# Heads' inverse root in a decoder block: one scale-and-add and one power on GpSimd in place of eleven chained VectorE operations

## The chip, the cores and the metric

One core of one Trainium2 chip runs the whole program. The metric is the device time in microseconds of one execution. A core has five engines with a queue each: TensorE (PE; its weight loads are listed as PEld), VectorE (DVE), ScalarE (ACT), GpSimd (POOL) and SyncE (SP), which here only issues transfers. Each engine works through its own queue in order; between engines the order is set by semaphores that the kernel writes out by hand.

## What is computed

A decoder block on x of shape (4, 256, 256): a decaying linear attention with 16 heads of 16 columns, then four routed experts, then a second small attention across the batch, each with a residual and a layer norm behind it. The part that matters here is the norm of each head behind the first attention:

```python
def _gated_group_rmsnorm(o, gate, weight):
    x = o * sigmoid(gate)
    xg = x.reshape(b, n, HEADS, HEAD_DIM)            # 16 heads of 16
    ms = mean(xg * xg, axis=-1, keepdims=True)
    xg = xg * rsqrt(ms + EPS)                        # EPS = 1e-6
    return xg.reshape(b, n, d) * weight
...
x = layernorm(x + gated_group_rmsnorm(attention) @ Wo)
x = layernorm(x + experts(x))
x = layernorm(x + second_attention(x))
```

## The kernel before, in words

The 1024 tokens lie as 8 tiles of 128 tokens, a token to a partition. The program is a software pipeline in rounds: in attention round i the engines work on tile i (scores), tile i-1 (weighted values) and tile i-2 (norm and output projection). Attention rounds are 0 to 7; rounds 8 and 9 finish the tiles 6 and 7 and already run beside the experts, whose rounds begin at round 7. Every engine has its own hand-written order within a round:

- **PE**, round i: `transpose_qk(i)`; `attend(i-1)` (L1106, L1111); in even rounds `make_state` (L1120); `proj_qkv(i+1)` (L1029); four matmuls `scores(i, g)` (L1087), of which the third and fourth wait until the first and second have been masked (their PSUM banks, 3 and 4, are used in turn); `transpose_on(i-2)` (L1024, reads the tile `on`); `turn_back(i-1)` (L1132); `project_o(i-2)` (L1029, reads `onT`, which ACT copies in L512). Then round i+1 begins with `transpose_qk`.
- **DVE**, round i: `copy_kT(i)` (L711); `gate_o(i-2)` (L733, makes `og`); `norm_o(i-2)`: the squares (L738), the sum over each head (L741, 128x16 into `oms`), and `inverse_root`; in even rounds `decay_state` (L726); `ln_apply` (L755); `rope_cos(i+1)` (L695); `mask_scores(i, 0)` and `(i, 1)` (L717); `rope_add(i+1)` (L704); `mask_scores(i, 2)` and `(i, 3)`; `residual1(i-2)` with its statistics (L762, L749, L751).
- **POOL**, round i: `sine_part(i+1)` (L284, two instructions, waits for ACT's L482); in round 7 one expert mask (L336); `scale_o(i-2)` (L292, makes `on` from `og` and `ors`); `ln_rstd(0, i-2)` (L298 and L301, an add and a power on one column); in rounds 1 to 3 `turn_keys(i)` (L317 to L326). In rounds 8 and 9 there is no sine part, and the expert masks (L336) stand behind `scale_o`.

`inverse_root` is a bit trick and three Newton steps: eleven instructions on 128x16, each waiting for the one before it through the semaphore `dve_chain`. Its last one raises `o_rstd`, on which `scale_o` waits. `inverse_root` is also called later, by `head_rstd`, on the second attention; that call isn't touched.

```python
link(eng.tensor_scalar(v, src, scale, eps, ALU.mult, ALU.add))
link(eng.tensor_scalar(dst.bitcast(I32), v.bitcast(I32), -0.5, float(0x5f3759df), ALU.mult, ALU.add))
for step in range(3):
    link(eng.scalar_tensor_tensor(out=a, in0=v, scalar=-0.5, in1=dst, op0=ALU.mult, op1=ALU.mult))
    link(eng.tensor_tensor(a, a, dst, ALU.mult))
    last = eng.scalar_tensor_tensor(out=dst, in0=a, scalar=1.5, in1=dst, op0=ALU.add, op1=ALU.mult)
```

Of the kernel before, what the change touches and what calls it, by code (L numbers as in the profile page):

```python
# [15 lines left out]
ALU = mybir.AluOpType  # L16
ACT = mybir.ActivationFunctionType
AX = mybir.AxisListType
# [3 lines left out]
P = 128  # L22
# [3 lines left out]
H, HD = 16, 16  # L26
# [5 lines left out]
LN_EPS, RMS_EPS = 1e-5, 1e-6  # L32
# [55 lines left out]
def decoder_block(nc, x, tokens, ctx, wq, wk, wv, wo, wg1, wg2, norm_w, conv_w, fwq, fwk, fwv, fwg, router, fwout,  # L88
                  consts, out):
    stack = ExitStack()  # L90
    with stack:
        def sb(name, shape, dt=F32):
            return stack.enter_context(nc.sbuf_tensor(name, shape, dt))
# [5 lines left out]
        def S_(name):  # L99

            if name not in made:
                made[name] = stack.enter_context(nc.semaphore(name))
            return made[name]
# [37 lines left out]
        oT = sb("oT", [P, 2, 512])  # L141
        og = sb("og", [P, 2, D])
        osq = sb("osq", [P, 2, D])
        oms = sb("oms", [P, H])
        ors = sb("ors", [P, 2, H])
        on = sb("on", [P, 2, D])
        onT = sb("onT", [P, 2, KT, P])
# [57 lines left out]
        half_neg = con[:, C_POW:C_POW + 1]  # L205
# [4 lines left out]
        def heads(ap, e=HD):  # L210
            return ap.rearrange("p (h e) -> p h e", e=e)
# [48 lines left out]
        def _(eng):  # L260
# [25 lines left out]

            def scale_o(i):

                eng.wait_ge(S_("o_rstd"), i + 1)
                if i >= 2:  # L290
                    eng.wait_ge(S_("onT_made"), i - 1)
                eng.tensor_tensor(heads(on[:, i % 2, :]), heads(og[:, i % 2, :]),  # L292
                                  ors[:, i % 2, :].unsqueeze(2).to_broadcast([P, H, HD]), ALU.mult)\
                   .then_inc(S_("o_normed"), 1)
# [46 lines left out]
            def attention_round(i):  # L341
                if i + 1 < TILES:
                    sine_part(i + 1)
                if i == MOE_START:
                    eng.wait_ge(S_("mask"), 6)
                    mask_part("hTe_pool", hTe, hT, 0, (VECTOR_EXPERTS_H, E), "z_made", "hT_copied")
                if 0 <= i - 2 < TILES:
                    scale_o(i - 2)
                    if i < TILES:
                        ln_rstd(0, i - 2)  # L350
                if 1 <= i < L:
                    turn_keys(i)
# [279 lines left out]
        def _(eng):  # L632
# [40 lines left out]
            def link(ins):  # L673
                chain[0] += 1
                ins.then_inc(S_("dve_chain"), 1)
                eng.wait_ge(S_("dve_chain"), chain[0])

            def inverse_root(dst, src, n, scale, eps, done):

                v, a = newton[:, 0, 0:n], newton[:, 1, 0:n]  # L680
# [6 lines that stand above are left out]
                    if step < 2:  # L687
                        link(last)
                last.then_inc(S_(done), 1)
# [46 lines left out]
            def norm_o(i):  # L736
                eng.wait_ge(S_("gated"), i + 1)
                eng.tensor_tensor(osq[:, i % 2, :], og[:, i % 2, :], og[:, i % 2, :], ALU.mult)\  # L738
                   .then_inc(S_("o_squared"), 1)
                eng.wait_ge(S_("o_squared"), i + 1)  # L740
                eng.tensor_reduce(oms[:, :], heads(osq[:, i % 2, :]), AX.X, ALU.add).then_inc(S_("o_ms"), 1)  # L741
                eng.wait_ge(S_("o_ms"), i + 1)
                if i >= 2:
                    eng.wait_ge(S_("o_normed"), i - 1)
                inverse_root(ors[:, i % 2, :], oms[:, :], H, 1.0 / HD, RMS_EPS, "o_rstd")

            def ln_stats(n, i, xin):
                eng.wait_ge(S_(f"ln{n}_sum"), i + 1)
# [32 lines left out]
            def attention_round(i):  # L781
# [11 lines left out]
                if 0 <= i - 2 < TILES:  # L793
                    gate_o(i - 2)
                    norm_o(i - 2)
# [563 lines left out]
```

## Time and profile before

| what | value |
|---|---|
| time, median of 3 runs | 255.02 us |
| lowest and highest run | 254.4 and 258.87 us |
| span of the profiled execution | 256.0 us |
| busy: PE, DVE, POOL, ACT | 209.2, 176.7, 114.0, 81.7 us |
| mean granted TensorE clock | 0.925 of full speed |
| instructions | 3809 |

The span runs from the first instruction to the last of one profiled execution; it is the time that the rows below add up to, 1.0 us above the median of the runs. A busy share is a mean over stages with different limits, so the stage around the change (here from about 42 to 148 us) has to be read by itself.

### The profile page before, as it was taken

How to read it: one execution, taken by the hardware profiler on the slowest of the kernel's cores; microseconds unless marked ns; L12 is line 12 of the kernel's file. 1: busy time of each engine (PE TensorE's matmuls, PEld its weight loads, DVE VectorE, ACT ScalarE, POOL GpSimd, SP SyncE). 2: the span in 40 equal slices, each digit the busy share in tenths (PEclk: the TensorE clock that was granted, in tenths of full speed). 3: DMA queues.
4: the chain of work that ended last, by engine and by line, in shares of the span. 5: the costliest groups of instructions: out<-in, count | busy, mean ns of one | idle time of the engine just before them, and what ended most of it. 6: DMA issues, size and time to landing. Idle time of an engine off the chain costs nothing.

```text
span 256.0 us, 3809 instructions
## 1 busy us (share of the span) xinstructions
PE 209.2 (82%) x1254; PEld 146.0 (57%) x1254; DVE 176.7 (69%) x438; ACT 81.7 (32%) x219; POOL 114.0 (45%) x188
## 2 busy tenths in 40 slices
PE   3788999995987798849799989999999997842461
PEld 1367555562745364515799776686786966411340
DVE  1168848779597979793556863348769788897751
ACT  0075664452432534241100113403223234423021
POOL 9661207335161413140516352346558529656352
PEclk9999999999799999977979999999999999995555
DMA  7990000000000000000000000000000001001011
GB/s 195 339 299 5 3 0 4 0 1 0 3 1 0 3 1 0 3 0 0 3 0 3 1 0 0 3 1 0 0 3 0 0 4 40 3 0 41 0 38 45
DMA packets 7027, 6.65 MB, mean 26 GB/s; under 512 B 1232, under 2 KB 6624, under 8 KB 7008
## 3 DMA queue, kind: packets, MB, share of 16 engines
q1 hardware_dynamic: 5744, 5.33, 6.6%
q10 hardware_dynamic: 1264, 1.08, 1.4%
q8 instruction: 10, 0.16, 0.3%
q14 instruction: 9, 0.07, 0.1%
HBM read 5.36 MB, written 1.05 MB: 25 GB/s over the span
## 4 chain that ended last, share of the span: by engine, by line
PE 52%; DVE 24%; issue 9%; POOL 6%; ACT 4%; DMA 3%; ACTq 1%; DVEq 0%; POOLq 0%
PE bank L1029 19%; PE bank L1230 12%; PE bank L1087 9%; PE bank L1244 4%; PE bank L1024 3%; DMA w_qk<-in_L_attn_Wk 3%; DVE hTe L776 2%; DVE w_qk L937 2%; PE bank L1132 2%; DVE stats L749 1%; POOL rstd L301 1%; DVE newton L685 1%; DVE probs L717 1%; PE bank L1120 1%; DVE newton L684 1%
## 5 line engine op out<-in xcount | busy, mean ns | idle before, releaser
L1087 PE MATMUL bank<-qx,kT 128*128 128x512 f32 x64 | 33.7, 652 | 10.6 <-DVE probs L717 8.9
L1230 PE MATMUL bank<-hTe,ctxT 128*128 128x128 f32 x256 | 31.7, 285 | 2.6 <-issue 2.6
L1230 PEld LDWEIGHTS bank<-hTe,ctxT 128*128 128x128 f32 x256 | 31.0, 201 | 3.2 <-issue 3.1
L499 ACT ACTIVATE qx<-bank,con 32x256 f32<-32x256 f32 x64 | 26.4, 458 | 16.0 <-PE bank L1024 15.4
L1244 PE MATMUL bank<-ctxT,aTe 128*128 128x256 f32 x128 | 29.0, 379 | 0.0
L284 POOL TENSOR_TENSOR rsin<-qk,rope_tab 128x256 f32<-128x256 f32 x16 | 13.2, 845 | 34.9 <-ACT qk L482 34.9
L1029 PE MATMUL bank<-f_w,oT 128*128 128x512 f32 (+4 forms) x80 | 28.0, 496 | 0.8 <-ACT oT L552 0.7
L298 POOL TENSOR_SCALAR rstd<-agg 128x1 f32<-128x1 f32 x24 | 5.3, 222 | 49.3 <-DVE agg L751 48.5
L1087 PEld LDWEIGHTS bank<-qx,kT 128*128 128x128 f32 x64 | 11.7, 197 | 26.8 <-issue 24.5
L717 DVE TENSOR_TENSOR probs<-bank,con 128x512 f32<-128x512 f32 x32 | 21.6, 686 | 5.8 <-PE bank L1087 5.0
L1244 PEld LDWEIGHTS bank<-ctxT,aTe 128*128 128x128 f32 x128 | 23.7, 190 | 2.9
L336 POOL TENSOR_TENSOR aTe<-rcos,mask 128x256 f32<-128x256 f32 x8 | 11.9, 1493 | 25.5 <-DVE rcos L835 25.5
L1029 PEld LDWEIGHTS bank<-f_w,oT 128*128 128x128 f32 x80 | 14.4, 190 | 12.0 <-issue 5.7
L835 DVE TENSOR_TENSOR rcos<-rcos,bank 128x256 f32<-128x256 f32 x8 | 3.4, 420 | 21.7 <-ACT rcos L602 21.7
L1029 PE MATMUL bank<-w_qk,xT 128*128 128x512 f32 x32 | 17.0, 658 | 1.5 <-DMA w_qk<-in_L_attn_Wk 1.5
L301 POOL TENSOR_TENSOR rstd<-rstd,con 128x1 f32<-128x1 f32 x24 | 14.0, 582 | 2.0
L336 POOL TENSOR_TENSOR hTe<-hT,mask 128x512 f32<-128x512 f32 x8 | 13.3, 1656 | 2.6 <-ACT hT L539 2.6
L1024 PE MATMUL bank<-con,fgo 128*128 128x128 f32 x16 | 3.7, 357 | 12.8 <-POOL fgo L414 12.8
L512 ACT ACTIVATE onT<-bank 128x256 f32<-128x256 f32 x8 | 3.1, 384 | 33.8 <-PE bank L1024 33.8
L1029 PE MATMUL bank<-f_out,onT 128*128 128x256 f32 x32 | 11.7, 522 | 1.6 <-ACT onT L592 1.6
L1024 PEld LDWEIGHTS bank<-con,fgo 128*128 128x128 f32 x16 | 2.4, 179 | 15.2 <-POOL fgo L414 14.8
L1111 PE MATMUL bank<-probs,v_sb 128*32 128x128 f32 x256 | 10.8, 274 | 0.0
(128 smaller groups left out, 407.7 us busy)
## 6 DMA issues: line engine op xcount, KB each, us to landing
x_sb<-in_x SPq DMA_DIRECT2D x4, 256.0 KB, 6.8
ctx_sb<-in_ctx SPq DMA_DIRECT2D x1, 1024.0 KB, 12.3
out<-x_sb SPq DMA_DIRECT2D x8, 128.0 KB, 1.7
fgo<-in_itok_BxS ACTq DMA_DIRECT2D x1, 512.0 KB, 9.3
con<-shape_constants SPq DMA_DIRECT2D x1, 338.5 KB, 3.0
w_v<-in_L_attn_Wv SPq DMA_DIRECT2D x1, 256.0 KB, 5.5
w_qk<-in_L_attn_Wq ACTq DMA_DIRECT2D x1, 256.0 KB, 5.7
w_qk<-in_L_attn_Wk ACTq DMA_DIRECT2D x1, 256.0 KB, 7.3
```

What stands on the lines that cost most here:

```text
L284: eng.tensor_tensor(dst[:, :, s, :], src[:, :, 1 - s, :], tab[:, :, s, :], ALU.mult)\
L298: eng.tensor_scalar(rstd[:, n, i:i + 1], agg[:, n, i, 1:2], LN_EPS, None, ALU.add)\
L301: eng.tensor_tensor(rstd[:, n, i:i + 1], rstd[:, n, i:i + 1], half_neg, ALU.pow)\
L336: eng.tensor_tensor(dst[:, j % 2, experts[0]:experts[1], :, :], two(src[:, j % 2, :]).unsqueeze(1).to_broadcast([P, n, KT, P]), mask[:, ex ...
L499: eng.activation(qx[rr, i % 2, :, 2 * r + par, :], two(bank[2][rr, 0:2 * P]), ACT.Copy, scale=con[rr, C_PARITY + par:C_PARITY + par + 1]). ...
L717: eng.tensor_tensor(probs[:, i % 2, 4 * g:4 * g + 4, :], bank[3 + g % 2][:, :].rearrange("p (h n) -> p h n", h=4), causal.unsqueeze(1).to_ ...
L1024: last = eng.transpose(dst[:, k * P:(k + 1) * P], src[:, k * P:(k + 1) * P], ident)
L1029: last = eng.matmul(dst, lhsT[:, k, :], w[:, k, :], start=(k == 0), stop=(k == KT - 1))
L1087: eng.matmul(bank[3 + g % 2][:, :], kT[:, i % 2, g // 2, :], qx[:, i % 2, g // 2, 4 * (g % 2):4 * (g % 2) + 4, :].rearrange("p h n -> p (h ...
L1111: last = eng.matmul(bank[5][32 * n:32 * n + 32, g * P:(g + 1) * P], v_sb[:, i % 3, h, :], probs[:, i % 2, h, :], start=(i % 2 == 0), stop= ...
L1230: last = eng.matmul(bank[0][:, f * P:(f + 1) * P], ctxT[:, k, e, f * P:(f + 1) * P], hTe[:, j % 2, e, k, :], start=(e == 0 and k == 0), st ...
L1244: last = eng.matmul(bank[3][:, 0:D], aTe[:, j % 2, e, k, :], ctxT[:, k, e, :], start=(e == 0 and k == 0), stop=(e == E - 1 and k == KT - 1))
```

## The change

The eleven operations leave VectorE. The sums of the squares, `oms`, get a second buffer, and VectorE's part ends with the sum, which raises `o_ms`. GpSimd's `scale_o` now waits for `o_ms` instead of `o_rstd`, scales and adds (`1/16` and the epsilon) into `ors`, waits for that, raises it to the power -0.5 with a column of constants spread over the 16 columns, waits for that, and then scales `og` as before. VectorE's sum waits, from the third tile on, for the power of the tile two before it.

```diff
-        oms = sb("oms", [P, H])
+        oms = sb("oms", [P, 2, H])
@@ def scale_o(i):   (GpSimd)
-                eng.wait_ge(S_("o_rstd"), i + 1)
+                eng.wait_ge(S_("o_ms"), i + 1)
+                eng.tensor_scalar(ors[:, i % 2, :], oms[:, i % 2, :], 1.0 / HD, RMS_EPS, ALU.mult, ALU.add)\
+                   .then_inc(S_("o_meansq"), 1)
+                eng.wait_ge(S_("o_meansq"), i + 1)
+                eng.tensor_tensor(ors[:, i % 2, :], ors[:, i % 2, :], half_neg.to_broadcast([P, H]), ALU.pow)\
+                   .then_inc(S_("o_rooted"), 1)
+                eng.wait_ge(S_("o_rooted"), i + 1)
                 if i >= 2:
                     eng.wait_ge(S_("onT_made"), i - 1)
                 eng.tensor_tensor(heads(on[:, i % 2, :]), heads(og[:, i % 2, :]),
@@ def norm_o(i):   (VectorE)
                 eng.wait_ge(S_("o_squared"), i + 1)
-                eng.tensor_reduce(oms[:, :], heads(osq[:, i % 2, :]), AX.X, ALU.add).then_inc(S_("o_ms"), 1)
-                eng.wait_ge(S_("o_ms"), i + 1)
                 if i >= 2:
-                    eng.wait_ge(S_("o_normed"), i - 1)
-                inverse_root(ors[:, i % 2, :], oms[:, :], H, 1.0 / HD, RMS_EPS, "o_rstd")
+                    eng.wait_ge(S_("o_rooted"), i - 1)
+                eng.tensor_reduce(oms[:, i % 2, :], heads(osq[:, i % 2, :]), AX.X, ALU.add).then_inc(S_("o_ms"), 1)
```

## Rows read from the trace of the kernel before

**Rows 1.** The page: busy time of each engine.

```profile
PE 209.2 (82%) x1254; PEld 146.0 (57%) x1254; DVE 176.7 (69%) x438; ACT 81.7 (32%) x219; POOL 114.0 (45%) x188
```

**Rows 2.** Stretches, rounds 2, 3, 5, 7, 8: length; PE, PEld, DVE, ACT, POOL busy; clock.

```profile
42.19:53.73 11.54, 11.39 (x101) 7.14 (x100) 8.73 (x24) 5.15 (x12) 3.79 (x8) 1.00 0.01 3
53.73:67.65 13.92, 11.09 (x63) 6.66 (x62) 10.65 (x25) 5.15 (x12) 5.68 (x13) 0.88 0.00 1
...
81.79:93.55 11.76, 9.68 (x63) 5.58 (x62) 9.86 (x25) 5.15 (x12) 2.94 (x5) 1.00 0.01 2
...
106.87:120.42 13.55, 10.14 (x57) 4.93 (x56) 9.22 (x24) 4.55 (x11) 3.05 (x4) 0.75 0.00 1
120.42:134.31 13.89, 11.92 (x137) 11.38 (x136) 7.92 (x21) 1.87 (x5) 4.57 (x5) 0.88 0.00 1
```

**Rows 3.** Waits of PE from 42 to 121: us in total, times, longest.

```profile
PE bank L1087 <- DVE probs L717: 8.9, 5, 2.8
```

**Rows 4.** Timeline of round 5: start, length, engine, line, tiles, [idle before].

```profile
83.19 0.22 POOL L298 TENSOR_SCALAR rstd<-agg 128x1 f32<-128x1 f32 x1 [5.28 <-DVE agg L751]
...
83.48 0.57 POOL L301 TENSOR_TENSOR rstd<-rstd,con 128x1 f32<-128x1 f32 x1
83.78 0.42 DVE L738 TENSOR_TENSOR osq<-og 128x256 f32<-128x256 f32 x1
...
84.69 0.17 DVE L681 TENSOR_SCALAR newton<-oms 128x16 f32<-128x16 f32 x1
...
87.20 0.65 DVE L686 SCALAR_TENSOR_TENSOR ors<-newton,ors 128x16 f32<-128x16 f32 x1
...
88.09 1.10 DVE L695 TENSOR_TENSOR rcos<-qk,rope_tab 128x512 f32<-128x512 f32 x1
...
89.94 1.96 PE L1087 MATMUL bank<-qx,kT 128*128 128x512 f32 x4 [2.04 <-DVE probs L717]
```

**Rows 5.** Timeline of round 2, where PE never waits.

```profile
48.15 3.85 PE L1087 MATMUL bank<-qx,kT 128*128 128x512 f32 x8
48.26 1.81 POOL L284 TENSOR_TENSOR rsin<-qk,rope_tab 128x256 f32<-128x256 f32 x2 [4.59 <-ACT qk L482]
...
50.03 0.61 POOL L292 TENSOR_TENSOR on<-og,ors 128x256 f32<-128x256 f32 x1
...
51.84 0.38 PE L1024 MATMUL bank<-con,on 128*128 128x128 f32 x2
```

**Rows 6.** GpSimd's groups by form: busy us, mean ns of one | idle before.

```profile
L301 POOL TENSOR_TENSOR rstd<-rstd,con 128x1 f32<-128x1 f32 x24 | 14.0, 582 | 2.0
...
L361 POOL TENSOR_SCALAR side<-fd 128x32 f32<-128x32 f32 x3 | 1.7, 555 | 0.2
...
L361 POOL TENSOR_SCALAR side<-fd 128x16 f32<-128x16 f32 x2 | 0.6, 320 | 0.1
...
L370 POOL TENSOR_TENSOR pick<-th,side 128x16 f32<-128x16 f32 x2 | 0.4, 221 | 0.0
L377 POOL TENSOR_SCALAR pick<-pick 128x16 f32<-128x16 f32 x2 | 0.4, 203 | 0.2
```

**Rows 7.** Timeline of rounds 7 to 9: slow scores and experts, `oms`, `on`.

```profile
114.97 3.75 PE L1087 MATMUL bank<-qx,kT 128*128 128x512 f32 x4 [1.55 <-DVE probs L717]
...
129.48 0.42 DVE L741 TENSOR_REDUCE oms<-osq 128x16 f32<-128x256 f32 x1
...
132.28 0.62 POOL L292 TENSOR_TENSOR on<-og,ors 128x256 f32<-128x256 f32 x1 [3.77 <-DVE ors L686]
...
134.31 0.38 PE L1024 MATMUL bank<-con,on 128*128 128x128 f32 x2
...
142.50 0.42 DVE L741 TENSOR_REDUCE oms<-osq 128x16 f32<-128x256 f32 x1
...
145.30 0.72 POOL L292 TENSOR_TENSOR on<-og,ors 128x256 f32<-128x256 f32 x1 [4.07 <-DVE ors L686]
...
146.10 0.42 PE L1024 MATMUL bank<-con,on 128*128 128x128 f32 x2
```

## The prediction

> **What bounds the kernel now.** I read the page first: TensorE is busy for 82% of the span, VectorE for 69%, GpSimd for 45% [rows 1]. So TensorE sets the time, and a shorter VectorE is worth something only where TensorE waits for it. The stretches by round show where: round 2 takes 11.5 us with 11.4 of TensorE work and full clock; round 3 takes 13.9 with less work and a clock of 0.88; round 7 takes 13.6 with a clock of 0.75 [rows 2]. The view of waits names the gap: from 42 to 121 us TensorE waits five times, 8.9 us in total, for `probs` (L717) before its third score matmul [rows 3]. The timeline of round 5 shows why: `inverse_root` occupies VectorE's queue from 84.69 to 87.85, and behind it `rope_cos` runs at 88.09, the masking of scores only then, and the third score matmul starts at 89.94 after an idle 2.04 us [rows 4]. The eleven instructions are on the path in rounds 3 to 7. In round 2 they lie under other TensorE work, and all four scores run through in 3.85 us [rows 5].
>
> **What is removed.** An uncontended step takes 0.17 us, one that meets GpSimd's sine part 0.65; the chain is 3.2 us long in round 5 [rows 4]. Without it VectorE reaches `rope_cos` before ScalarE has made its input, and the round's middle looks like round 2. So all of the 8.9 us of waiting goes. After the longer waits TensorE ran at a lower clock: two score matmuls took 3.75 us in round 7 [rows 7] where they take 1.96 in round 5 [rows 4], 1.8 us more; round 3 has a clock of 0.88 over 13.9 us [rows 2], which is 1.7 us. Together 3.5 us that go as well. Removal is worth 8.9 + 3.5 = 12.4 us. In rounds 8 and 9 TensorE is filled with the experts (11.9 of 13.9 us busy [rows 2]), so the chain's removal there is costed at nothing: experts' matmuls hide it.
>
> **What is added.** On GpSimd, in front of each `on`: a scale-and-add and a power on 16 columns, each with a wait for its own completion. A scale-and-add of 16 columns takes 0.20 us, a product of two 16-column tiles 0.22 [rows 6]; between one GpSimd instruction and one that depends on it lies a little under 0.1 us (83.41 to 83.48 [rows 4]), which I round up. The price of the power on 16 columns, p, isn't in the trace, and everything hangs on it. The only power there is has one column: 0.58 us in the mean, 0.57 typically [rows 4, 6], so 0.35 us above a plain product of 16 columns.
> - Low end: all of those 0.35 us are paid once per instruction. Then p is about 0.6.
> - High end: they are paid for each column. Then p = 0.2 + 16 x 0.35 = 5.8.
>
> Which is nearer? The nearest row on growth with columns is the comparison L361: 0.32 us at 16 columns, 0.555 at 32 [rows 6], 15 ns a column, where the plain instructions next to it hardly grow. That is an operation that the engine doesn't do at a plain product's rate, and its cost grows by the column. A power is a far longer calculation of the same kind, and I see no sign that the parts for different columns overlap. I take most, not all, of the 0.35 as per column: 0.27, and so p = 0.2 + 16 x 0.27 = 4.5 us. This is a choice between 0.6 and 5.8, and the weakest step here.
>
> The Trainium skill (GPSIMD Engine Reference, Elementwise — side-by-side cycle accounting) gives about 2.6 cycles per element for a two-input operation at 1.2 GHz. By that figure 16 columns cost an estimated 35 ns over the one-column price, p would be 0.6, and the sum would come out at the fast case below. Its Instruction dispatch section calls the instruction an ordinary loop over elements, which alone decides nothing about a power's body. No row here shows either for a power.
>
> **Where the power lies.** GpSimd's queue in round i is: sine part, then scale, power and `on`. In round 2 the sine part ends at 50.07, and TensorE begins to transpose `on` at 51.84, so with the weight load ahead of it wants it at about 51.7 [rows 5]. New: 50.07 + 0.1 + 0.2 + 0.1 + p + 0.1 + 0.7 (the product L292, from 0.61 to 0.72 [rows 5, 7]) = 51.3 + p. TensorE therefore waits d = p - 0.4 in each of the rounds 2 to 7, at a new place: in front of `transpose_on`. Behind it in TensorE's queue stand the transposes back, the output projection and the next round's `transpose_qk`, so all of d moves the next round. With p = 4.5, d = 4.1, six times: 24.6 us. In round 3 `turn_keys` delays the sine part, and in round 7 the expert mask stands before `scale_o`: 1.3 us more together.
>
> Rounds 8 and 9: `oms` is ready at 129.90; `on` would be there at 129.90 + 0.5 + 4.5 + 0.65 = 135.5, and TensorE transposes it at 134.31: 1.2 us. In round 9: 142.92 + 0.5 + 4.5 + 0.75 = 148.7 in place of 146.02 [rows 7]: 2.6 us. The expert masks on GpSimd behind it are late by the same time, and the experts' matmuls wait for them.
>
> Clock: rounds 3 (a gap of 2.8 us [rows 3]) and 7 had a slower stretch that cost 1.7 or 1.8 us (above); the gap of round 5, 2.04 us [rows 4], left none (clock 1.00 [rows 2]). Six gaps of 4.1 us cost 1.5 each: 9 us.
>
> **Sum** for p = 4.5: -12.4 + 24.6 + 1.3 + 1.2 + 2.6 + 9 = +26 us on the profile's 256.0, so 282. The profile lies 1.0 us above the median of the runs, so 281 us.
>
> VectorE's new wait, for the power of the tile two before, is costed at nothing: that power is over a round earlier. Were it not, `oms` and the masking behind it would be late. The second `oms` buffer costs nothing. No transfer is touched.
>
> **Rivals.**
> 1. *The power is nearly flat in columns* (p = 0.6 to 1.4). For: the 0.35 us may be a fixed entry. Against: L361's growth. At p = 1.0: -12.4 + 6 x 0.6 + 1.3 = -7.5, so 248.5, by the median 247.5 us; at 0.6, 245. The sign is on the other side of the forecast, and it decides at one point: without clock losses the sum is zero at p = 2.25.
> 2. *One wait takes the place of the other* (p = 1.4 to 2.9). TensorE no longer waits for `probs` but about as long for `on`: -12.4 + 6 x 1.6 + 1.3 = -1.5 at p = 2.0, so 253.5 us. For: if columns overlap in groups. VectorE is idler, the time is the same.
> 3. *A long power shuts VectorE out.* If the power kept a shared port for its whole length, `rope_add` (L704, two inputs in SBUF) would wait, and the product `on` would then queue with it. In round 5 the square L738, two reads from SBUF, runs at 83.78 in its usual 0.42 us in the middle of a one-column power (83.48 to 84.05) [rows 4]. So the trace speaks against it, for one column at least. It would add about 0.7 us a round, 4 us in all: 285 us. The Trainium skill (SBUF — State Buffer, SBUF: two separate sides) has such a lock between GpSimd and VectorE instructions with two SBUF inputs, held for the whole instruction. By that rule the square should have been held up; the trace does not agree.
> 4. *The removal gives less than 8.9 us*: `rope_cos` now starts beside the sine part, and may run in 1.10 us [rows 4] where I count on about 0.7. That takes at most 0.5 us a round, 2.5 us in all, in every case; it is in the range, not a case of its own.
>
> **Chances.** Steep power (p from 2.9 to 5.8): 0.45, with 262 to 292 us. The lock with it: 0.05, 285. In between: 0.15, 248 to 261. Nearly flat: 0.35, 244 to 249. About 2% (5 us) is what a measurement of this kernel can tell from no change. Slower 0.50, same 0.15, faster 0.35. Since cases of both signs hold most of the chance, the range covers them: 245 to 292 us; the likeliest case's own range is 262 to 292.
>
> **What would show it.** In the changed profile: the duration of the power's line on 128x16, first of all. Then TensorE's wait for `probs` before L1087, from 8.9 us to under 1 if the removal is read rightly; a new wait of L1024 or its weight load for `on`, of p - 0.4 us in rounds 2 to 7; the clock by round; and the length of rounds 2 to 7, 78 us now (42.19 to 120.42 [rows 2]), which grows or shrinks with p. The forecast is wrong if the power takes less than 2.25 us; it is wrong in another way if the wait for `probs` stays although the chain is gone.

## The result and the profile after

The changed kernel takes 264.1 us (median of 4 runs, 263.86 to 264.82), the kernel before beside it 254.82. The ratio is 1.034, 95% interval 1.029 to 1.040: slower, as forecast, but by 9 us and not by 26. 264.1 lies in the range given; the amount forecast for the loss was nearly three times too large. Executions that were clearly slower than the rest of their kernel (up to 317.4 us for the kernel before, 477.9 us for e1) stay out of the ratios.

The two traces differ by 7.0 us in span (256.0 and 263.0), the medians by 9.3. A span leaves out about 1.8 us of the time of an execution (264.82 us and 263.0 for the profiled one here), so the profiled execution of the kernel before, with 256.0 us and a mean clock of 0.925, lay nearer 3 us above its median than the 1.0 us that the table of before gives. The balance below is one of the two traces and explains their 7.0 us; the other 2.3 us lie between executions.

From the page of the changed kernel come the busy times and the two groups that tell most. The power on 16 columns stands there with 2.96 us in the mean.

```profile
PE 212.8 (81%) x1254; PEld 147.2 (56%) x1254; DVE 157.0 (60%) x350; ACT 81.6 (31%) x219; POOL 138.8 (53%) x204
...
L293 POOL TENSOR_TENSOR ors<-ors,con 128x16 f32<-128x16 f32 x8 | 23.7, 2957 | 0.7
...
L1028 PE MATMUL bank<-con,on 128*128 128x128 f32 x16 | 3.7, 316 | 13.9 <-POOL on L298 13.9
```

VectorE lost 20 us of work (176.7 to 157.0 [rows 1]), GpSimd gained 25, and TensorE, which sets the time, is busy for 3.6 us more. Where the time went shows in the waits of TensorE in the changed kernel from 42 to 128 us, rounds 2 to 7 (us in total, times, longest):

```profile
PE bank L1028 <- POOL on L298: 13.1, 6, 3.5
PE bank L1091 <- ACT qx L505: 1.7, 1, 1.7
PE bank L1124 <- DVE kT L717: 1.1, 1, 1.1
```

The 8.9 us for `probs` [rows 3] are gone from this view (round 7 has more to it, see e5). In their place TensorE waits 13.1 us, once in each of the six rounds, for `on`. The same stretches as in [rows 2], of the changed kernel (rounds 2 to 7; length; PE, PEld, DVE, ACT, POOL busy; clock):

```profile
42.08:55.96 13.88, 11.60 (x100) 7.05 (x99) 6.89 (x13) 5.14 (x12) 6.97 (x10) 1.00 0.01 2
55.96:70.53 14.57, 11.10 (x63) 6.52 (x62) 6.87 (x14) 5.14 (x12) 9.59 (x15) 0.89 0.01 2
70.53:86.57 16.04, 12.79 (x100) 7.82 (x99) 9.59 (x21) 5.14 (x12) 9.77 (x15) 0.93 0.00 0
86.57:100.15 13.58, 11.42 (x63) 6.45 (x62) 6.82 (x14) 5.14 (x12) 6.34 (x7) 0.88 0.00 1
100.15:114.83 14.68, 12.37 (x99) 7.52 (x98) 9.17 (x20) 5.14 (x12) 6.57 (x7) 0.95 0.01 1
114.83:127.35 12.52, 9.49 (x57) 4.60 (x56) 7.18 (x13) 4.55 (x11) 6.29 (x6) 0.86 0.00 1
```

Rounds 2 to 7 took 78.23 us before and take 85.27 now. Everything behind them is unchanged; one answer for each kernel gives both halves, first of the kernel before, then of the changed one:

```profile
42.19:120.42 78.23, 65.28 (x476) 38.74 (x475) 61.96 (x161) 30.31 (x71) 25.80 (x48) 0.93 0.00 1
120.42:256.00 135.58, 109.27 (x623) 85.75 (x621) 91.79 (x239) 34.63 (x114) 68.39 (x115) 0.90 0.03 9
```

```profile
42.08:127.35 85.27, 68.77 (x476) 39.97 (x475) 46.52 (x95) 30.27 (x71) 45.53 (x60) 0.92 0.00 1
127.35:263.00 135.65, 109.23 (x623) 85.73 (x621) 87.55 (x217) 34.62 (x114) 73.44 (x119) 0.90 0.03 9
```

The balance of the +7.04 us: waits for `on` +13.1, waits for `probs` -8.9, waits for `kT` in rounds 4 and 6 -0.9 (2.0 to 1.1), and 3.5 us by which the same 476 matmuls take longer (65.28 to 68.77). The sum is +6.8 of the +7.04. That the longer matmuls are a matter of the clock is seen in e5 below, where the same 476 take 62.08 us at a clock of 1.00.

One round of the changed kernel, the fifth, shows the mechanism (timeline):

```profile
89.06 0.42 DVE L749 TENSOR_REDUCE oms<-osq 128x16 f32<-128x256 f32 x1
...
91.42 3.85 PE L1091 MATMUL bank<-qx,kT 128*128 128x512 f32 x8
91.52 1.82 POOL L284 TENSOR_TENSOR rsin<-qk,rope_tab 128x256 f32<-128x256 f32 x2 [2.65 <-ACT qk L488]
...
93.42 0.20 POOL L290 TENSOR_SCALAR ors<-oms 128x16 f32<-128x16 f32 x1
93.71 2.91 POOL L293 TENSOR_TENSOR ors<-ors,con 128x16 f32<-128x16 f32 x1
93.94 0.68 DVE L710 TENSOR_TENSOR qkr<-rcos,rsin 128x512 f32<-128x512 f32 x1
...
96.70 0.62 POOL L298 TENSOR_TENSOR on<-og,ors 128x256 f32<-128x256 f32 x1
97.37 0.44 PE L1028 MATMUL bank<-con,on 128*128 128x128 f32 x2 [2.10 <-POOL on L298]
```

All four score matmuls run through in 3.85 us, as in round 2 of the kernel before [rows 5]: the middle of the round is now as the prediction drew it. The sums `oms` are ready at 89.48, but GpSimd first waits, idle, for the input of its sine part until 91.52, does that, and only then begins the root. TensorE is through with the scores at 95.27 and waits 2.10 us for `on`. GpSimd's idle 2.65 us between 88.87 and 91.52 is nearly the length of the power, and this gave the idea for e4 below.

### The profile page after: what moved, and what is told of

Its sections match the earlier page's. It is cut to its first block, busy times and chain, and to the rows that moved or that the text cites. A ratio compares the mean times of both kernels' runs of the same rounds, so it can differ in the third digit from the quotient of the medians.

```text
span 263.0 us, 3737 instructions
## 1 busy us (share of the span) xinstructions
PE 212.8 (81%) x1254; PEld 147.2 (56%) x1254; DVE 157.0 (60%) x350; ACT 81.6 (31%) x219; POOL 138.8 (53%) x204
## 4 chain that ended last, share of the span: by engine, by line
PE 45%; POOL 22%; DVE 15%; issue 8%; ACT 6%; DMA 3%; ACTq 1%; POOLq 0%; DVEq 0%
PE bank L1033 20%; PE bank L1234 10%; POOL ors L293 8%; PE bank L1028 4%; POOL rsin L284 3%; PE bank L1091 3%; DMA w_qk<-in_L_attn_Wk 3%; PE bank L1248 3%; DVE w_qk L941 2%; DVE hTe L780 2%; POOL rstd L307 2%; POOL on L298 2%; PE bank L1124 2%; PE bank L1136 1%; DVE stats L753 1%
## 5 line engine op out<-in xcount | busy, mean ns | idle before, releaser
L1091 PE MATMUL bank<-qx,kT 128*128 128x512 f32 x64 | 32.5, 632 | 1.8 <-ACT qx L505 1.7
L284 POOL TENSOR_TENSOR rsin<-qk,rope_tab 128x256 f32<-128x256 f32 x16 | 14.2, 905 | 34.7 <-ACT qk L488 34.7
L505 ACT ACTIVATE qx<-bank,con 32x256 f32<-32x256 f32 x64 | 26.3, 458 | 18.7 <-PE bank L1028 18.1
L293 POOL TENSOR_TENSOR ors<-ors,con 128x16 f32<-128x16 f32 x8 | 23.7, 2957 | 0.7
L342 POOL TENSOR_TENSOR aTe<-rcos,mask 128x256 f32<-128x256 f32 x8 | 11.2, 1401 | 23.6 <-DVE rcos L839 23.6
L766 DVE TENSOR_TENSOR x<-bank,x_sb 128x256 f32<-128x256 f32 x8 | 3.4, 420 | 23.9 <-PE bank L1033 23.9
L1028 PE MATMUL bank<-con,on 128*128 128x128 f32 x16 | 3.7, 316 | 13.9 <-POOL on L298 13.9
L1028 PE MATMUL bank<-con,fgo 128*128 128x128 f32 x16 | 3.7, 357 | 12.9 <-POOL fgo L420 12.9
## 6 DMA issues: line engine op xcount, KB each, us to landing
x_sb<-in_x SPq DMA_DIRECT2D x4, 256.0 KB, 6.6
w_v<-in_L_attn_Wv SPq DMA_DIRECT2D x1, 256.0 KB, 5.4
w_qk<-in_L_attn_Wq ACTq DMA_DIRECT2D x1, 256.0 KB, 5.9
w_qk<-in_L_attn_Wk ACTq DMA_DIRECT2D x1, 256.0 KB, 7.0
```

Of the source, the lines that this page charges most:

```text
L284: eng.tensor_tensor(dst[:, :, s, :], src[:, :, 1 - s, :], tab[:, :, s, :], ALU.mult)\
L293: eng.tensor_tensor(ors[:, i % 2, :], ors[:, i % 2, :], half_neg.to_broadcast([P, H]), ALU.pow)\
L342: eng.tensor_tensor(dst[:, j % 2, experts[0]:experts[1], :, :], two(src[:, j % 2, :]).unsqueeze(1).to_broadcast([P, n, KT, P]), mask[:, ex ...
L505: eng.activation(qx[rr, i % 2, :, 2 * r + par, :], two(bank[2][rr, 0:2 * P]), ACT.Copy, scale=con[rr, C_PARITY + par:C_PARITY + par + 1]). ...
L1028: last = eng.transpose(dst[:, k * P:(k + 1) * P], src[:, k * P:(k + 1) * P], ident)
L1091: eng.matmul(bank[3 + g % 2][:, :], kT[:, i % 2, g // 2, :], qx[:, i % 2, g // 2, 4 * (g % 2):4 * (g % 2) + 4, :].rearrange("p h n -> p (h ...
```

## The experiments

All ratios are to the kernel before, from runs on the same chip; the number in brackets is the 95% interval. The median of the kernel before differs from group to group (254.8 to 257.0 us), so kernels of different groups are compared by their ratios. The theory T is the prediction's: only two things in a round cost TensorE time, the masking that comes late behind the chain and the `on` that comes late behind the power; what engines do elsewhere is free.

**e1_no_root: the removal alone.** Scale-and-add and power are left out, so the heads are scaled by their plain sums of squares.

```diff
                 eng.wait_ge(S_("o_ms"), i + 1)
-                eng.tensor_scalar(ors[...], oms[...], 1.0 / HD, RMS_EPS, ALU.mult, ALU.add)
-                eng.tensor_tensor(ors[...], ors[...], half_neg.to_broadcast([P, H]), ALU.pow)
                 eng.tensor_tensor(heads(on[:, i % 2, :]), heads(og[:, i % 2, :]),
-                                  ors[:, i % 2, :].unsqueeze(2)...
+                                  oms[:, i % 2, :].unsqueeze(2)...
```

> Against the changed kernel, the scale-and-add and the power are left out, so the heads are multiplied by their plain sums of squares; only the order and the time matter. It is the removal alone. Theory T (TensorE's wait for probs goes, nothing takes its place): the 8.9 us of waits and about 3.5 us of lower clock go from the kernel before, so about 243 to 244 us, ratio 0.955. Rival (the eleven operations were mostly hidden, and only part of the wait comes back because rope_cos then meets the sine part): 249 us or more, ratio over 0.975, and a remaining wait of TensorE for probs of over 3 us.

Measured: 245.3 us, ratio 0.954 (0.949 to 0.959). The removal is worth 11.7 us (10.4 to 12.9 by the interval), against 12.4 in the prediction. Its only trace is of the execution of 477.9 us and isn't read here; e5 stands in for the waits.

**e2_power_8, e5_power_1, e3_power_twice: the power's length.** The same kernel with the power on 8 columns, on one (the other heads keep their mean square), and with a second, equally long power in front of it.

```diff
# e2, and e5 with 0:1
-                eng.tensor_tensor(ors[:, i % 2, :], ors[:, i % 2, :], half_neg.to_broadcast([P, H]), ALU.pow)
+                eng.tensor_tensor(ors[:, i % 2, 0:8], ors[:, i % 2, 0:8], half_neg.to_broadcast([P, 8]), ALU.pow)
# e3
+                eng.tensor_tensor(spare[:, i % 2, :], ors[:, i % 2, :], half_neg.to_broadcast([P, H]), ALU.pow)\
+                   .then_inc(S_("o_spare"), 1)
+                eng.wait_ge(S_("o_spare"), i + 1)
                 eng.tensor_tensor(ors[:, i % 2, :], ors[:, i % 2, :], half_neg.to_broadcast([P, H]), ALU.pow)
```

> Against the changed kernel, the power is taken on 8 of the 16 columns; the other heads keep the mean square, so they are scaled wrongly. Two questions. The power's price by column: 2.91 us at 16 columns and 0.57 at one give 0.157 us a column; a straight line gives 1.66 us at 8, a price in groups or a threshold gives something else. The time: with TensorE's wait for on at the power's length less 0.4 us, six times, theory T gives 256.0 - 12.4 + 6 x 1.25 + 1.3 = 252.4 on the profile, ratio about 0.985. Rival (GpSimd's added occupation itself costs, whatever stands behind it): the same saving per us in all eight rounds, 264.1 - 8 x 1.25 = 254, ratio 0.997 or more.

> Against the changed kernel, the power is taken on one of the 16 columns; the other heads keep the mean square. It is the price that a power flat in columns would have had, 0.57 us, and so the low end of the prediction run as a kernel. Theory T: -12.4 + 6 x 0.2 + 1.3 = -9.9, about 246 us, ratio 0.96; TensorE's wait for on under 2 us in all, the clock near that of the kernel before or better. With the 16, 8 and doubled powers it gives the time against the power's length at four lengths; theory T has a slope of about 6 to 8 from 1.7 us on and less below. Rival (GpSimd's occupation costs by itself): a slope of 8 all along, which from 253.6 at 1.66 us gives 245 too, so the profile's waits, not the time, tell them apart here.

> Against the changed kernel, the power runs twice, once into a spare tile, each waited for: 5.9 us in place of 2.91, with 0.1 us between. Theory T: all of the added 3.0 us in rounds 2 to 7 (18 us), 2.5 us in round 8 and 2.9 in round 9, and longer gaps with a lower clock: 264.1 + 23.4 = 287.5 us, up to 292 with clock, ratio 1.13 to 1.145. It also tests the sum of the prediction at the price that it took for the high end. Rival (the wait is partly hidden, or another engine's work takes up slack): under 280 us, ratio under 1.10.

Measured, with the changed kernel in its place (TensorE's waits for `on` over the whole run, from the view of waits):

| power in front of `on` | length, us | time, us | ratio (95% interval) | TensorE waits for `on`, us |
|---|---|---|---|---|
| one column (e5) | 0.55 | 246.9 | 0.963 (0.955 to 0.971) | 1.6 |
| 8 columns (e2) | 1.66 | 253.6 | 0.991 (0.987 to 0.995) | 6.4 |
| 16 columns (changed kernel) | 2.91 | 264.1 | 1.034 (1.029 to 1.040) | 13.9 |
| 16 columns twice (e3) | 5.9 | 295.9 | 1.155 (1.149 to 1.161) | 38.6 |

The tile view has the lengths (ns shortest/median/longest), first of e2, then of e3; the third fence is from the view of waits of e3 (us in total, times, longest):

```profile
L293 POOL TENSOR_TENSOR ors<-ors,con x8: 1647/1658/2177, 50.8 to 140.5; 128x8 f32<-128x8 f32 x8
```

```profile
L294 POOL TENSOR_TENSOR spare<-ors,con x8: 2906/2908/3227, 49.8 to 175.8; 128x16 f32<-128x16 f32 x8
L297 POOL TENSOR_TENSOR ors<-ors,con x8: 2895/2897/2911, 52.8 to 178.8; 128x16 f32<-128x16 f32 x8
```

```profile
PE bank L1032 <- POOL on L302: 38.6, 8, 6.1
```

On the 255 us of before, the ratios give 245.6, 252.7, 263.7 and 294.5 us. Per us of power that is 6.4 us between the first two, 8.8 between the next, and 10.3 between the last. By the intervals the first slope is uncertain by about 2 us and the second by 1.4, so these two are not clearly apart. The reading that goes with T is six rounds at first, then rounds 8 and 9 (eight waits in e3) and a lower clock (0.961 in e5, 0.920 in the changed kernel, 0.894 in e3). The 10.3 is more than the eight places at which a power stands; e3's expected top of 292 us was exceeded. The ratio of e2 lies between what T (0.985) and its rival (0.997 or more) had; the waits speak for T, for all five of e2's waits for `on` fall in rounds 2 to 6 and none in rounds 8 and 9. The line crosses 255 us at 1.66 + 2.3 / 8.8 = 1.9 us of power, between 9 and 10 columns. Between 2.91 and 5.9 us a straight line puts a power of 4.5 at 263.7 + 1.6 x 10.3 = 280 us. That is an estimate, no kernel had it; by it the prediction's sum of 281 was about right for the price that it had put in.

The trace of e5 shows rounds 2 to 7 with only 1.6 us of waits behind the power. First come these rounds and all that follows, then round 7, in which a wait for `probs` is left although the chain is gone.

```profile
41.64:111.20 69.56, 62.08 (x476) 36.27 (x475) 46.39 (x95) 30.31 (x71) 32.30 (x60) 1.00 0.01 1
111.20:244.00 132.80, 107.16 (x623) 84.17 (x621) 87.95 (x217) 34.63 (x114) 70.02 (x119) 0.93 0.03 9
```

```profile
104.88 0.69 DVE L780 TENSOR_TENSOR hTe<-hT,mask 128x512 f32<-128x512 f32 x1 [1.92 <-ACT hT L545]
105.49 1.35 DVE L759 TENSOR_SCALAR h<-x,agg,rstd 128x256 f32<-128x256 f32 x1
...
107.59 1.95 PE L1091 MATMUL bank<-qx,kT 128*128 128x512 f32 x4 [1.67 <-DVE probs L723]
```

Here VectorE waits for ScalarE's `hT`, masks an expert and then does `ln_apply` (L759) before it gets to the scores. The same wait of 1.7 us stands in e2 and e3. In the changed kernel it doesn't show, because all four scores run slowly there (5.63 us from the first to the last, where e5 takes 5.60 with the wait in it).

**e4_root_first: the same power, earlier in GpSimd's queue.**

```diff
             def attention_round(i):      # GpSimd
+                if 0 <= i - 2 < TILES:
+                    scale_o(i - 2)
                 if i + 1 < TILES:
                     sine_part(i + 1)
...
                 if 0 <= i - 2 < TILES:
-                    scale_o(i - 2)
                     if i < TILES:
                         ln_rstd(0, i - 2)
```

> Against the changed kernel, only the order of GpSimd's queue: scale_o (scale-and-add, power, product) stands before the sine part of the next tile. The sums are ready 1.5 to 2.3 us before ScalarE has the input of the sine part, so the power runs in GpSimd's idle time. The power is as long as before. Theory T (what costs is only that on comes late for TensorE): the wait for on nearly goes in rounds 4 to 7, about 1.2 us stay in round 3 behind turn_keys; rope_add comes later but before TensorE's next transposes: 246 to 249 us, ratio 0.97. Rival P (a power of 2.9 us costs wherever it stands, by occupying GpSimd or by holding VectorE's two-input operations off): no gain over the changed kernel, 262 us or more, ratio 1.03. Rival S (the late sine part moves the wait to transpose_qk and the late masks): 255 us or so, ratio 1.0.

Measured: 249.9 us, ratio 0.974 (0.971 to 0.978). The power is as long as before (2917 ns in the tile view), its place is worth 14 us (15 by the ratios). Timeline of round 5 in this kernel:

```profile
82.53 2.91 POOL L293 TENSOR_TENSOR ors<-ors,con 128x16 f32<-128x16 f32 x1
83.29 3.85 PE L1092 MATMUL bank<-qx,kT 128*128 128x512 f32 x8
...
85.52 0.62 POOL L298 TENSOR_TENSOR on<-og,ors 128x256 f32<-128x256 f32 x1
86.10 1.40 POOL L284 TENSOR_TENSOR rsin<-qk,rope_tab 128x256 f32<-128x256 f32 x2
86.98 0.38 PE L1029 MATMUL bank<-con,on 128*128 128x128 f32 x2
...
87.59 0.69 DVE L711 TENSOR_TENSOR qkr<-rcos,rsin 128x512 f32<-128x512 f32 x1 [1.69 <-POOL rsin L284]
```

`on` is ready at 86.14, TensorE takes it at 86.98 without a wait. The sine part comes later by the root's length and VectorE waits for it (1.69 us). In this round that costs TensorE nothing; over rounds 2 to 7 it is not quite free, for TensorE's waits for `kT` are 3.2 us here, 1.1 in the changed kernel and 2.0 before. A wait for `on` of 1.8 us is left in round 3, where T had 1.2, and the time is just above T's 246 to 249 us. Rival P, that a power costs by occupying GpSimd, falls. So does rival S in its amount (255 us), while part of its mechanism is in those 3.2 us.

**e6_both: the power added, nothing removed.**

```diff
                 eng.tensor_reduce(oms[:, i % 2, :], heads(osq[:, i % 2, :]), AX.X, ALU.add).then_inc(S_("o_ms"), 1)
+                eng.wait_ge(S_("o_ms"), i + 1)
+                inverse_root(spare[:, i % 2, :], oms[:, i % 2, :], H, 1.0 / HD, RMS_EPS, "o_rstd")
```

> Against the changed kernel, VectorE's eleven operations are put back as well, into a tile that nothing reads, so that the power is added and nothing is removed. Theory T (both waits hang on one place in TensorE's order: a TensorE held up before its third score matmul wants on that much later, and the power runs meanwhile): 2 us in round 2, 1 us each in rounds 4 and 6, next to nothing in 3, 5 and 7, 1 us in round 9: 260 to 262 us, ratio 1.02, and the wait for probs stays at about 9 us. Rival A (the two costs add up): the kernel before plus what the power costs with the chain gone, 264.1 - 245.3 = 18.8 us: 274 us, ratio 1.07.

Measured: 262.3 us, ratio 1.022 (1.014 to 1.030). The two costs don't add up: with the chain gone the power costs 264.1 - 245.3 = 18.8 us (20 by the ratios), with the chain there 5.6 by the ratio. Waits of TensorE in e6, from 38 to 165 us:

```profile
PE bank L1031 <- POOL on L299: 7.1, 7, 2.1
PE bank L1094 <- DVE probs L724: 6.6, 5, 2.0
```

In round 3 it waits 1.96 us for `probs` and then only 0.22 for `on`; in round 5 1.62 and 0.82. A TensorE that is held up early in the round asks for `on` that much later. That is also why this change, in its order, could not collect the removal's 12 us: taking away the first wait exposes the second. The wait for `probs` was expected to stay at 9 us and fell to 6.6. The chain isn't shorter for it (3.94 and 3.15 us in rounds 3 and 5, 3.93 and 3.16 before). But `rope_cos` behind it now runs beside the power, where it ran beside the product `on` (in round 4 the sine part), and takes 0.68 to 0.70 us in rounds 3 to 5 where it took 1.10 to 1.21 [rows 4]. Round 5 of e6:

```profile
90.58 0.68 DVE L702 TENSOR_TENSOR rcos<-qk,rope_tab 128x512 f32<-128x512 f32 x1
90.80 3.22 POOL L294 TENSOR_TENSOR ors<-ors,con 128x16 f32<-128x16 f32 x1
```

That is all of the 0.42 us by which round 5's wait fell, and half of the 0.87 in round 3; in round 4 a longer chain took it back. The 0.96 us of round 7 come from slower scores ahead of the wait (3.36 us for 2.70) and from a masking that follows the chain sooner.

**e8_chain_scale_first: VectorE's chain as before, only GpSimd's order changed** (the diff of e4, on the kernel before).

> The kernel before with VectorE's chain, and only GpSimd's order changed as in the kernel with the root first: the product on ahead of the sine part. Theory T: on was not late in the kernel before, so nothing is won; the sine part now waits for the chain's end, which lies 0.4 us or more behind ScalarE's result in rounds 3 and 5, so the same or 1 to 2 us slower: 255 to 258 us. Rival (the order alone brings the gain of the root-first kernel, the power has no part in it): 250 us, ratio 0.975.

Measured: 252.4 us, ratio 0.984 (0.977 to 0.992). Neither expectation: T had it the same or slower, the rival at 250. TensorE's waits for `probs` fell from 8.9 us [rows 3] to 6.7:

```profile
PE bank L1088 <- DVE probs L718: 6.7, 5, 1.9
```

The timeline of round 5 of e8 shows the end of the chain:

```profile
84.49 0.17 DVE L687 SCALAR_TENSOR_TENSOR ors<-newton,ors 128x16 f32<-128x16 f32 x1
...
84.75 0.72 POOL L292 TENSOR_TENSOR on<-og,ors 128x256 f32<-128x256 f32 x1 [2.99 <-DVE ors L687]
```

Its last steps take 0.17 us where they took up to 0.65 beside the sine part [rows 4]; the chain of that round is 2.3 us long (82.40 to 84.66) in place of 3.2. In round 3 the chain is 0.95 us shorter too. In round 7, where there is no sine part, the kernel before has the expert mask on GpSimd beside the chain's last step, and e8 has it behind `on`. The kernel before:

```profile
111.70 1.26 POOL L336 TENSOR_TENSOR hTe<-hT,mask 128x512 f32<-128x512 f32 x1 [2.57 <-ACT hT L539]
...
111.86 1.14 DVE L686 SCALAR_TENSOR_TENSOR ors<-newton,ors 128x16 f32<-128x16 f32 x1
```

The waits for `probs` fell by 0.95, 0.88 and 1.16 us in rounds 3, 5 and 7, and rose by 0.42 in each of rounds 4 and 6, where `on` and the sine part now meet `ln_apply` on VectorE (0.82 us in round 4, 0.40 before). Some of what the prediction booked to the eleven operations was GpSimd's work running into them.

**e7_tidy and e9_tidy_chain: the last waits, with the power and without.** On top of e4 (e7) and of e8 (e9): on GpSimd `turn_keys` goes ahead of `ln_rstd`; on VectorE the one-off work on the second attention's weights (rounds 3 and 5) goes from the end of the round to the gap ahead of `rope_add`.

```diff
# GpSimd
+                if 1 <= i < L:
+                    turn_keys(i)
                 if 0 <= i - 2 < TILES:
                     if i < TILES:
                         ln_rstd(0, i - 2)
-                if 1 <= i < L:
-                    turn_keys(i)
# VectorE
                 for g in range(4):
                     if i < TILES:
                         mask_scores(i, g)
+                    if g == 1:
+                        prepare(i)      # the blocks "if i == 3" and "if i == 5", moved here
                     if i + 1 < TILES and g == 1:
                         rope_add(i + 1)
```

> Against the kernel with the root ahead of the sine part: on GpSimd turn_keys goes ahead of ln_rstd, into the gap behind the sine part; on VectorE the one-off preparation of the weights (rounds 3 and 5) goes from the end of the round to the gap ahead of rope_add. Left there were a wait for on of 1.8 us in round 3 and waits of make_state for kT of 2.0 and 1.2 us in rounds 4 and 6. Theory T (TensorE sets the time and these are its last waits in this stage): 245 to 247 us, ratio to the kernel before 0.96. Rival (the stage is now bound otherwise, the waits move on to attend or to transpose_qk): 249 us or more.

> The orders of e7_tidy, but with the root as VectorE's chain of eleven, as in the kernel before: it tells what the power itself is worth once the orders are the same. Theory T: e8_chain_scale_first (252.4) less the waits for kT of 2.0 us: 250 to 251 us, TensorE's waits for probs stay near 6.7 us, ratio 0.978; so the power's part in the gain of e7_tidy is about 5 us. Rival (in good orders the chain is hidden too, and the power is worth nothing): 246 us, ratio 0.96.

Measured: e7 245.0 us, ratio 0.954 (0.947 to 0.961); e9 248.2 us, ratio 0.970 (0.965 to 0.976). The two intervals don't meet, so in good orders the power is worth about 1.6%, 3 to 4 us, and e7 beats both the kernel before and the changed one. For e9 neither expectation holds: T had 0.978, the rival 0.96. TensorE's waits in rounds 2 to 7 of e7:

```profile
PE bank L1096 <- ACT qx L506: 1.7, 1, 1.7
PE bank L1033 <- DVE qkr L711: 0.2, 1, 0.2
PE bank L1033 <- DVE kT L718: 0.2, 1, 0.2
```

Neither `probs` nor `on` is left in these rounds (1.9 us for `on` stay in rounds 8 and 9). In e9 5.4 us of waits for `probs` remain. 1.3 of them are in round 7, where e5 waits 1.67 without a chain, so the chain's own part in the waits is nearer 4 us.

**e10_probe: the power by columns, and beside VectorE.** Behind the last work of the changed kernel stand single powers, and then powers beside a train of VectorE products with two SBUF inputs.

```diff
+            eng.memset(probe[:, :], 2.0).then_inc(S_("probe"), 1)
+            for w in (1, 2, 4, 8, 16, 32, 64):      # then mult on 1, 16, 64; then pow on 16, 64 beside VectorE
+                eng.tensor_tensor(res[:, 0:w], probe[:, 0:w], half_neg.to_broadcast([P, w]), ALU.pow)
...
+            for n in range(36):                     # VectorE
+                link(eng.tensor_tensor(osq[:, 0, :], og[:, 0, :], og[:, 1, :], ALU.mult))
```

> The changed kernel with probes behind its last GpSimd and VectorE work, so its span is longer by 20 us or more: on GpSimd powers of 2.0 on 1, 2, 4, 8, 16, 32 and 64 columns, products of the same operands on 1, 16 and 64, then powers on 16 and 64 again while VectorE multiplies two SBUF tiles of 256 columns, 36 times. Expected for a straight line through 0.57, 1.65 and 2.91 us: 0.73, 1.04, 1.67, 2.92, 5.4, 10.5 us at 2 to 64 columns. A price in groups of four would show equal values at 1, 2 and 4. Port theory (a power keeps VectorE's two-input operations off for its length): a product of VectorE beside the power on 64 columns takes up to 10 us. Rival, by the row of the changed kernel: each stays at 0.43 us, with at most a short delay of either at the start.

GpSimd's groups by form in e10, from 262 to 303 us (busy us, mean ns | idle before); L479 alone, L489 beside VectorE, L484 the products. The second fence has VectorE's train in the tile view (ns shortest/median/longest). The probe ran once, and only its durations are read:

```profile
L489 POOL TENSOR_TENSOR res<-probe,con 128x64 f32<-128x64 f32 x1 | 10.8, 10762 | 0.1
L479 POOL TENSOR_TENSOR res<-probe,con 128x64 f32<-128x64 f32 x1 | 10.5, 10522 | 0.1
...
L479 POOL TENSOR_TENSOR res<-probe,con 128x16 f32<-128x16 f32 x1 | 2.9, 2895 | 0.1
...
L479 POOL TENSOR_TENSOR res<-probe,con 128x2 f32<-128x2 f32 x1 | 0.7, 705 | 0.1
L479 POOL TENSOR_TENSOR res<-probe,con 128x1 f32<-128x1 f32 x1 | 0.6, 559 | 0.1
L484 POOL TENSOR_TENSOR res<-probe,con 128x64 f32<-128x64 f32 x1 | 0.3, 295 | 0.1
...
L484 POOL TENSOR_TENSOR res<-probe,con 128x1 f32<-128x1 f32 x1 | 0.2, 193 | 0.1
```

```profile
L1045 DVE TENSOR_TENSOR osq<-og x36: 424/426/426, 286.3 to 302.4; 128x256 f32<-128x256 f32 x36
```

The price is a straight line from one column to 64: about 0.40 us and 0.157 us a column. The second column already costs 0.146 more, so nothing is done in groups of columns. All 36 products of VectorE take 0.424 to 0.426 us, beside a power of 10.8 us too; the power itself is 0.24 us longer. The port theory falls for a power. For GpSimd's products it is another matter: beside the expert mask above, a 16-column step of VectorE that takes 0.17 us alone took 1.14, to the mask's end.

## Why the prediction was right or wrong

*What bounds the kernel, and what the removal is worth: right in place and size, in part by luck.* The wait for `probs` went from 8.9 us to none in rounds 2 to 7, and the removal alone gave 11.7 us for 12.4. But not all of the 8.9 us were the chain's. In round 7 1.7 us of wait are there without it (e5), and 2.2 us went by an order alone, where GpSimd's sine part and expert mask had met the chain's last steps (e8). Against that the removal gave something behind round 7, which the prediction had at nothing: 132.80 us in e5 for 135.58, at a clock of 0.93 for 0.90.

*The price of the power: the step that failed.* The prediction had 0.57 us at one column, took 0.35 of it as dearer than a plain product, gave 0.27 to the column, and wrote p = 4.5 between the ends 0.6 and 5.8. Measured: 2.91. Of the 0.56 us at one column 0.40 are paid once and 0.157 by the column; a plain product pays about 0.19 once and 1.6 ns a column. So of the 0.35 us above the product more than half is an entry that the power pays once per instruction. The idea taken from L361, that the cost grows by the column without overlap, was right; the split of one column's price could not be read from one column, and the value chosen was 1.5 times the true one. Put into the prediction's own terms without its clock term, p = 2.91 gives -12.4 + 6 x 2.5 + 1.3 + 1.0 = +4.9 us. That is 260.9 us on the scale of the spans, where 263.0 was measured. At other lengths the same terms give 246 us for 0.55 (span of e5: 244.0), 252.4 for 1.66 (e2: 252.1) and 284.6 for 5.9 (e3: 292.8). So without the clock they hold to about 2 us up to 2.91 and are 8 short at 5.9. From the forecast +26.3 to the +7.0 of the traces, the price of the power makes 12.4 us in the terms of the waits (9.6 in six rounds, 2.8 in rounds 8 and 9). The rest is smaller: 3.2 for the wait in front of `transpose_on`, 2.0 for the clock, 1.0 for round 9 and 0.9 for the waits for `kT`.

*The wait in front of `transpose_on`, d = p - 0.4: right in place, a little large.* 2.51 x 6 + 1.3 = 16.4 us forecast by it for this p, 13.1 measured: 2.10 in round 5, 3.45 in round 3, but 1.17 in round 7, where TensorE waited for ScalarE first (L505, 1.7 us, as in the kernel before) and was late with its scores.

*Rounds 8 and 9: wrong at this p.* Round 9 waited 0.8 us for `on`, as the terms would have it, but the stretch behind round 7 is as long as before (135.58 and 135.65 us). By these lengths that wait cost nothing later on. At 5.9 us of power both rounds waited about 4 us.

*The clock: right in kind, too large.* The prediction took away 3.5 us and added 9, net +5.5. The same 476 matmuls of rounds 2 to 7 took 65.28 us before, 62.08 in e5 with most of the waits gone, and 68.77 in the changed kernel: 3.2 us given back, 6.7 added, net +3.5. The 9 us were for gaps of 4.1 us, the gaps were 1.2 to 3.5. Its rule of thumb, that a gap of 2 us leaves no slower stretch, fell: round 5 has a gap of 2.10 us at its new place and a clock of 0.88, where a gap of 2.04 left 1.00 [rows 2]. What decides it was not tested.

*The rivals.* Nearly flat (1) falls by e10. One wait in the place of the other (2) is what happened in kind, at a p that tips it over: the point of no change was put at 2.25 us of power and lies at 1.9. The lock (3) falls: in the changed kernel `rope_add` starts 0.23 us after the power and takes its usual 0.68 us, and e10 has it over 10 us. The Trainium skill (SBUF — State Buffer, SBUF: two separate sides) has the pair held for the whole instruction; for a GpSimd power no run here agrees. Rival (4), that `rope_cos` loses to the sine part, didn't come about: it takes 0.69 us in rounds 2 to 6 of the changed kernel, and TensorE's scores run through.

The Trainium skill (GPSIMD Engine Reference, Elementwise — side-by-side cycle accounting) gives about 2.6 cycles per element for two inputs, at its 1.2 GHz an estimated 2.2 ns a column. The product agrees in size: (295 - 193) / 63 = 1.6 ns a column. The power, with 157 ns a column, is a hundred times that.

## What to carry to other kernels

An operation's price at one column says nothing about its price by the column: before moving an elementwise function from one column to sixteen, time it at two widths. When a chain is taken off one engine, look at which wait stands next in the queue of the engine that sets the time; here it was in the same round, and the gain and the new wait could not be added up one by one. And where a new long operation goes in its own queue matters about as much as its length: the same change, with 2.9 us of power, cost 9 us with the power behind an instruction that waits for another engine, and gained 6 us with it in front.

## What the runs showed of the hardware

GpSimd's power is 0.40 us and 0.157 us a column, in a straight line to 64 columns (10.5 us), while its product takes 0.19 to 0.30 us over the same widths. A power of 10.8 us on GpSimd left VectorE's two-input products at 0.426 us each. GpSimd's sine part, in contrast, stretched VectorE's 16-column steps from 0.17 to 0.65 us [rows 4], and its expert mask of 512 columns one such step to 1.14 us (111.86 in the kernel before). An order that keeps most of them apart went with a ratio of 0.984 (0.977 to 0.992, e8). The same 476 matmuls took 62.08 us at a granted clock of 1.00 (e5) and 68.77 at 0.92 (changed kernel).
